# Fewer shapes of the matmul array: spreads on 64 rows, a last layer on 128 rows, and some fp32 matmuls cut into strips

## The reference

```
x = group_norm(x); q,k,v = 1x1 convs(x); x = softmax(q k^T * s) v, projected, + x      # layer 0, one head, 1024 x 1024 scores
h = group_norm(x); q,k,v with 8 heads of 16; x = concat(softmax(q k^T) v) wp + x       # layer 1, eight heads
h = instance_norm(x); q,k,v = 1x1 convs(h); x = x + softmax(q k^T * s) v               # layer 2, one head
Q,K (16 channels), V = 1x1 convs(x); Qn,Kn = l2norm over channels                      # layer 3, linear attention
out = gamma * (sum_n V + Qn (Kn V)) / (N + Qn . (sum_n Kn + eps))
```

## Time and profile before

| | us |
|---|---|
| median of 3 runs | 6187.2 |
| the runs | 6186.3 to 6193.7 |
| the profiled execution, its own time | 6179.8 |
| its span (first to last instruction) | 6178.0 |

### The profile page before, as it was taken

The page is one execution under the profiler, slowest core; times in us unless marked ns, Lnnn a source line. Parts: engine busy times, 40 slices in busy tenths (PEclk is TensorE's granted clock), DMA queues, the critical chain, the costliest instruction groups (busy, mean ns, idle before and its releaser), DMA issues.

```text
span 6178.0 us, 82441 instructions
## 1 busy us (share of the span) xinstructions
PE 5741.7 (93%) x28818; PEld 2690.0 (44%) x28818; DVE 4620.2 (75%) x5748; ACT 4141.6 (67%) x5764; POOL 3426.0 (55%) x2739
## 2 busy tenths in 40 slices
PE   5789999999999999999999999999999999999885
PEld 2334444444444444444444444444444444444332
DVE  2677777777777777777777777777777777777752
ACT  2367777766777676777766767767677777677652
POOL 4336655556665555655555666555565555566433
PEclk7899999999999999999999999999999999999996
DMA  1011101011101101111101110110110110111000
GB/s 36 4 27 24 29 21 30 20 31 24 31 19 30 31 20 31 24 25 25 29 21 31 24 31 19 30 30 21 31 24 21 29 30 20 31 24 31 16 17 8
DMA packets 103485, 154.27 MB, mean 25 GB/s; under 512 B 63776, under 2 KB 66080, under 8 KB 102944
## 3 DMA queue, kind: packets, MB, share of 16 engines
q1 hardware_dynamic: 103072, 149.00, 11.1%
HBM read 18.13 MB, written 16.78 MB: 6 GB/s over the span
## 4 chain that ended last, share of the span: by engine, by line
PE 72%; DVE 16%; ACT 5%; issue 3%; POOL 3%; DMA 0%; SPq 0%; DVEq 0%; POOLq 0%; ACTq 0%
PE p_max L1251 16%; PE p_chain L1251 15%; PE p_sc L1251 12%; PE p_full L1251 11%; PE p_acc L1251 9%; PE p_head L1251 8%; DVE mx_half L1066 8%; ACT p L930 3%; DVE f2mx L1061 2%; DVE fp L1107 2%; POOL x L787 1%; POOL fsum L781 1%; POOL fp_lo L760 1%; DVE f_num L1125 1%; DVE t_dn L1198 1%
## 5 line engine op out<-in xcount | busy, mean ns | idle before, releaser
L1066 DVE TENSOR_REDUCE mx_half<-p_max 128x2 f32<-128x1024 f32 x2048 | 2506.8, 1224 | 891.1 <-PE p_max L1251 883.1
L930 ACT ACTIVATE p<-p_head 128x1024 f32<-128x1024 f32 x2048 | 2094.8, 1023 | 1103.0 <-PE p_head L1251 1047.8
L760 POOL TENSOR_TENSOR fp_lo<-fp,fp_hi 128x512 fp32r<-128x512 f32 x1024 | 1311.6, 1282 | 734.1 <-ACT fp L894 732.5
L781 POOL TENSOR_TENSOR fsum<-fsum,fp 128x512 f32<-128x512 f32 x768 | 987.9, 1286 | 282.3 <-ACT fp L894 282.1
L1251 PE MATMUL p_max<-ks,qs 63*128 63x512 f32 x4096 | 993.9, 481 | 102.0 <-DVE mx_half L1066 80.3
L1251 PE MATMUL p_acc<-p,v 128*17 128x512 f32 x8192 | 1080.9, 601 | 7.8 <-ACT p L930 7.6
L1251 PE MATMUL p_head<-qs,ks 64*128 64x512 f32 x4096 | 938.9, 454 | 43.6 <-ACT p L930 26.5
L892 ACT ACTIVATE fp_hi<-fp 128x512 fp32r<-128x512 f32 x1024 | 641.4, 626 | 367.3 <-DVE fp L1107 261.6
L1107 DVE TENSOR_TENSOR fp<-p_sc,f_shifts 128x512 f32<-128x512 f32 x1024 | 700.1, 684 | 147.5 <-PE p_sc L1251 60.3
L1251 PEld LDWEIGHTS p_max<-ks,qs 63*128 63x128 f32 x4096 | 385.8, 185 | 921.5 <-DVE mx_half L1066 736.3
L1251 PEld LDWEIGHTS p_head<-qs,ks 64*128 64x128 f32 x4096 | 385.7, 185 | 679.5 <-issue 385.8
(11 more groups left out here) (187 smaller groups left out, 7977.6 us busy)
## 6 DMA issues: line engine op xcount, KB each, us to landing
qs<-cq_hi SPq DMA_DIRECT2D x128, 256.0 KB, 4.8
ks<-ck_hi SPq DMA_DIRECT2D x128, 256.0 KB, 4.7
x_in<-x_dram SPq DMA_DIRECT2D x32, 512.0 KB, 4.4
qs<-cq_lo SPq DMA_DIRECT2D x64, 256.0 KB, 4.4
ks<-ck_lo SPq DMA_DIRECT2D x64, 256.0 KB, 5.1
out_dram<-x SPq DMA_DIRECT2D x32, 512.0 KB, 5.3
o<-o SPq DMA_DIRECT2D x256, 32.0 KB, 2.0
zrow<-rz SPq DMA_DIRECT2D x128, 16.0 KB
```

Of the source, the lines that this page charges most:

```text
L760: pool.tensor_tensor(fp_lo[u % 2][:, :], fp[u % 2][:, :], f32(fp_hi[u % 2][:, :]), ALU.subtract).then_inc(f.plo, 1)
L781: pool.tensor_tensor(dst, dst, fp[u % 2][:, :], ALU.add).then_inc(f.sum, 1)
L930: act.activation(p1[slot][:, 2 * pr:2 * pr + 2, :], P_HEAD[:, :].rearrange("p (e n) -> p e n", e=2), ACT.Exp, scale=float(DH) ** -0.5).the ...
L1066: dve.reduce_max(mx_half[:, pr, :, t, kh], P_MAX[:, :].rearrange("p (e n) -> p e n", e=2), AX.X)\
```

## The change

1. `f_spread` and `o_spread` now take 64 rows (the rest of zrow and of the weights `spread_r` is zero), in the same shape as `m_max` and `s_scores`. Both one-head layers share one row (64) of zrow, so `f_return` waits for the other layer's last spread.
2. The last layer: `t_matrix` computes its 17x129 result four times, into the four column strips. `t_turn` transposes four token tiles at once (each padded to 32 columns), so it is two full matmuls of 128 columns and one use of P_CHAIN, and `t_turned` is one copy. A new POOL step `t_spots` makes four masked copies of the matrix, 128x512, and `t_out` is four full matmuls of 128 columns for each half.
3. `mm32`: a full fp32 matmul is issued as four matmuls on the four column strips where the matmul ahead of it was in column strips, and as before elsewhere.
4. P_SC gets a counter of reads like P_CHAIN's.
5. All of TIME is new, with PERIOD 205.92 instead of 206.0.

```diff
-FULL_ROW = {0: 64, 2: 96}
-PERIOD = 206.000
+SUM_ROW = HEAD_ROWS
+STRIP = 32
+PERIOD = 205.920
...
-    m_max=[-78.166, -74.172, -72.387, -66.848, -65.308, -64.707, -61.817, -60.589, -58.987,
...
+            def mm32(dst, lhsT, rhs):
+                if tiling[0] != "columns":
+                    return mm(dst, lhsT, rhs)
+                for j in range(C // STRIP):
+                    strip = slice(STRIP * j, STRIP * (j + 1))
+                    last = mm(dst[strip, :], lhsT[:, strip], rhs, tiles="columns")
+                return last
...
             def o_spread(b, h):
-                mm(P_CHAIN[:, :], spread_r[:, :], zrow[0:SPREAD, half(h)]).then_inc(sem.o_rb, 1)
+                mm(P_CHAIN[:, :], spread_r[0:HEAD_ROWS, :], zrow[0:HEAD_ROWS, half(h)], tiles="rows")\
+                    .then_inc(sem.o_rb, 1)
...
             def f_spread(b, h, layer):
-                f, r = full(layer), slice(FULL_ROW[layer], FULL_ROW[layer] + 2)
+                f, r = full(layer), slice(HEAD_ROWS, 2 * HEAD_ROWS)
-                mm(P_CHAIN[:, :], ones_r[r, :], zrow[r, half(h)]).then_inc(f.rb, 1)
+                mm(P_CHAIN[:, :], spread_r[r, :], zrow[r, half(h)], tiles="rows").then_inc(f.rb, 1)
...
             def t_matrix(b):
                 for t in range(T):
-                    last = mm(P_CHAIN[0:D3 + 1, 0:C + 1], ka[:, t, :], tm[:, t, 2 * D3:W3 + 1],
-                              start=t == 0, stop=t == T - 1)
+                    for j in range(G1):
+                        last = mm(P_CHAIN[STRIP * j:STRIP * j + D3 + 1, 0:C + 1], ka[:, t, :],
+                                  tm[:, t, 2 * D3:W3 + 1], start=t == 0, stop=t == T - 1,
+                                  tiles="columns")
...
-            def t_turn(b, h):
-                for t in range(T // 2):
-                    last = mm(P_CHAIN[0:D3 + 1, tile(t)], t_dn[:, 4 * h + t, :], mat("ident"))
+            def t_turn(b):
+                for h in range(2):
+                    last = mm32(P_CHAIN[:, tile(h)],
+                                t_dn[:, 4 * h:4 * h + 4, :].rearrange("p t d -> p (t d)"),
+                                mat("ident"))
...
             def t_out(b, h):
-                mm(P_CHAIN[:, :], ma[:, 0:C], qt3[:, 4 * h:4 * h + 4, :]).then_inc(sem.t_o, 1)
+                pe.wait_ge(sem.t_sp, b.at(PER.t_sp, 1))
+                for j in range(G1):
+                    last = mm32(P_CHAIN[:, tile(j)], ma_spots[:, j, :], qt3[:, h, :])
+                last.then_inc(sem.t_o, 1)
...
+            def t_spots(b):
+                pool.wait_ge(sem.chain, chain_left("t_keep", b))
+                pool.tensor_tensor(ma_spots[:, :, :],
+                                   ma.rearrange("p (a c) -> p a c", a=1).broadcast_to([C, G1, C]),
+                                   strips[:, :].rearrange("p (j a) -> p j a", a=1)
+                                   .broadcast_to([C, G1, C]), ALU.mult).then_inc(sem.t_sp, 1)
```

More of the change, by code:

```diff
@@ L54 @@
     t_project=(range(3),), t_tokens=(range(3),), t_norms=(), t_keys=(), t_matrix=(), t_keep=(),
-    t_ksum=(), t_scale=(), t_turn=(range(2),), t_turned=(range(2),), t_out=(range(2),),
+    t_spots=(), t_ksum=(), t_scale=(), t_turn=(), t_turned=(), t_out=(range(2),),
     t_leave=(range(2),), store=())
 TIME = dict(
[L59 to L64, removed]
@@ new lines @@
+    o_recip=[602.088, 671.352],
+    o_return=[498.504, 562.776],
+    o_move=[489.144, 552.48],
+    o_spread=[669.48, 671.04],
+    o_divide=[675.72, 679.464],
+    o_project=[674.472, 677.28],
+    o_residual=[682.584, 686.016],
+    i_stat=[689.448],
+    i_apply=[690.384],
+    f_out=[823.608],
+    t_project=[835.152, 837.96, 839.52],
+    t_tokens=[828.6, 832.032, 834.528],
+    t_norms=[837.648],
+    t_keys=[842.64],
+    t_matrix=[854.496],
+    t_keep=[845.76],
+    t_spots=[855.12],
@@ L181 @@
+    t_ksum=[856.056],
+    t_scale=[848.256],
+    t_turn=[863.856],
+    t_turned=[858.864],
+    t_out=[865.728, 869.472],
+    t_leave=[867.6, 868.848],
+    store=[798.648])
 CHAIN_READER = dict(g_average="g_var", p_average="p_var", f_qk="f_hi", p_qk="p_hi",
@@ L250 @@
     f_base = 2
-    f_based = 2
-    f_less = 2 * T
     f_sc = 2 * T
@@ L325, in __init__ @@
         self.base = new(f"f{layer}_base")
-        self.based = new(f"f{layer}_based")
-        self.less = new(f"f{layer}_less")
         self.sc = new(f"f{layer}_sc")
@@ L881, in f_exp @@
                 f = full(layer)
-                act.wait_ge(f.less, b.at(PER.f_less, u + 1))
+                act.wait_ge(sem.sc_read, sc_left("f_less", b, u, layer))
                 if u >= 2:
@@ L1286, in f_value @@
                 for t in range(T // 2):
-                    last = mm(P_CHAIN[:, tile(t)], src[:, tile(4 * h + t)],
+                    last = mm32(P_CHAIN[:, tile(t)], src[:, tile(4 * h + t)],
                               mat("wv0" if layer == 0 else "wv2"))
@@ L1300, in p_value @@
                 for t in range(T // 2):
-                    last = mm(P_CHAIN[:, tile(t)], hx[:, tile(4 * h + t)], mat("wv1"))
+                    last = mm32(P_CHAIN[:, tile(t)], hx[:, tile(4 * h + t)], mat("wv1"))
                 last.then_inc(sem.p_v, 1)
@@ L1320, in m_max @@
                     r = head_rows(e, SHIFT_ROW)
-                    last = mm(P_MAX[:, half(e)], qs[r, pr, tile(t)], ks[r, pr, half(kh)])
+                    last = mm(P_MAX[:, half(e)], qs[r, pr, tile(t)], ks[r, pr, half(kh)],
+                              tiles="rows")
                 last.then_inc(sem.m_s, 1)
```

328 lines of the change are left out of this document (177 added, 151 removed), and 48 rows, old and new, of tables (m_max, m_max_read, s_exp, s_scores).

## The result

| | median us | runs | range |
|---|---|---|---|
| before | 6187.2 | 19 | 6181.1 to 6193.7 |
| after | 6199.4 | 19 | 6177.5 to 6213.5 |

After against before is 1.0019, 95% interval 1.0013 to 1.0026: 0.19% slower, where the forecast was 1% faster. 6,199 lies outside the predicted range. The runs of after also differ more among each other (36 us) than those of before (13 us).

What follows compares the result with a forecast made beforehand. The prediction took PE as the bound. Shapes -75, transposes -41 and waits +46 gave -70 us, counted as -59 in the middle and -5 at the ends: 6,187.2 to 6,123 us, range from a little under 6,071 to 6,190.

Steps and rivals of the forecast that it cites:

- The new order's waits: PE's waits for readers of PSUM tiles, mainly P_MAX: shortfalls rise from 365 to 404, costing +46 us.
- Shapes and transposes: On PE, fewer changes of shape save 75 us and the last layer's four-token t_turn saves 41 us.
- Waits: The +46 us term for PE's waits on PSUM readers, scaled from waits seen of 13.3 us per image.
- t_matrix, t_out, mm32, t_spots, t_keep: Last-layer steps, fp32 strips and the new POOL step: each taken to add 0 us.
- A: Rival for the whole kernel: all 116 us come through and waits don't grow, 6,071 us; chance 0.17.
- B: Rival: DVE's reads of P_MAX set the pace, time stays at 6,187 or reaches 6,232 us; chance 0.19.
- C: Rival: t_matrix is bound by issue at 0.077 us a pass, 6,224 us; chance 0.06 together with D.
- D: Rival: strips of mm32 run one after the other, +160 us, 6,283 us; chance 0.06 together with C.
- The case's own range: The main forecast's narrower range, 6,092 to 6,152 us, explained as half of +46 more or none of it.

Runs made afterwards that it cites:

- e1: The changed kernel with one number moved, so VectorE takes o_recip(1) after m_neg(0) and one f_less instead of ahead of them: 6127.1 us.
- e4: The changed kernel with every fp32 matmul of mm32 in one piece, none in column strips: 6221.4 us.
- e7: e1 with every fp32 matmul of mm32 in one piece, none in column strips: 6154.7 us.
- e14: e2 with every fp32 matmul of mm32 in one piece, none in column strips: 6160.3 us.
- e2: The changed kernel's code with the whole time table of the kernel before: 6154.2 us.
- e5: The changed kernel with the first m_max of the second half moved behind f_pv(11): 6208.6 us.
- e6: e1 with the first m_max of the second half moved behind f_pv(11): 6158.5 us.
- e3: The kernel before with o_recip(1) taken ahead of one f_less and m_neg(0) on VectorE: 6247.5 us.
- e9: The changed kernel with o_recip(1) behind m_neg(0), one f_less and the second half's first mx_half, and both o_spread later: 6145.1 us.

## Why the prediction was wrong

**The step that failed is "The new order's waits".** I summed, for each PSUM tile, how far the next use on PE stands from the last, and took that for all that a new order can do. I had sums over the PSUM tiles and none over the transfers: nothing asked where in DVE's order `o_recip(1)` now stands against `m_neg(0)`, although the order of that engine was there to be read. The earlier trace rows held its tile's waits alone. Two things are missing there, 72 us together. The first is the wait for the gather of `zt`, 1.88 us of DVE's time in the image shown and up to 29 us of the total. The second has no term at all in the prediction: I read "full granted clock" in the earlier trace rows as a property of the middle, and a new order can lose it. Its loss made the other 43 us or more. With that one number moved (e1) the kernel took 6127.1 where 6,123 was forecast, and 180.6 us between most stores, which is what 182.8 less 2.2 gives.

**That agreement is in part two errors that cancel.** *Shapes and transposes:* -116 forecast, 3.6 us per image. PE's busy time fell by 2.5 per image (176.0 to 173.5), about -80. The experiments put most of the excess on the price of a change of shape, 0.07 to 0.17 us instead of 0.20. That figure came from distances between starts in one stretch of a timeline; that a change costs less where PE waits anyway may be the reason, and wasn't tested. *Waits:* +46 forecast for the middle and ends, 1.4 per image; PE's idle time rose from 6.9 to 7.5, about +19. PE's own waits in the middle rose from 130 to 151 us. The scale of this term was a remainder, too: 13.3 us of waits per image, where by the earlier trace rows PE is idle for 6.9.

*t_matrix, t_out, mm32, t_spots, t_keep:* 0 forecast for all. `t_matrix` 1.77 as forecast; POOL's `t_spots` is waited for by nobody. PE's wait for `t_dn`, 16.5 us in the middle of before, is gone in after and e1; the prediction had seen it and set it against a cost of `t_keep`. e4, e7 and e14 say that the strips save what their shapes save, or a little more.

**Rivals.** A (full gain) didn't come in any kernel. B was nearest in kind: it gave DVE's queue as the way to a slower kernel, `f_less` held up behind an earlier entry. It named P_MAX's reads as that entry, at 109 us. The real one was an entry that waits for a DMA. Its probability of slower was 0.07. C is refuted by the rows of `t_matrix`, D by the strips' 1.04 us for a group.

**The chances.** I gave 0.13 to slower. Every case had been worked out at a constant clock, so no range could hold what happened. The case's own range, 6,092 to 6,152, doesn't follow from the reason given for it either: half of +46 more gives 6,146, and none of it 6,077.

## To carry to other kernels

When an order is changed, look on every engine for an entry that waits for a transfer and has moved ahead of one that the bounding engine needs; a sum over tiles doesn't see it. Read a full clock as a state that the present order keeps up, and put a price on its loss wherever a change lets TensorE stand for a microsecond or two in every image. Before a new order is judged, move such an entry back by itself: here one number of over 600 was worth more than the rest of the change.

## What the runs showed of the hardware

**The clock.** In before, e2 and e14 TensorE's clock stayed at 2.4 GHz for the whole middle. In after it fell behind stands of 0.2 to 0.7 and 1.6 to 2.1 us, the starts behind them 3 to 3.5 us apart, in nearly every image; in e5 behind one of 2.3 to 2.4 us in nearly every image, and in e6 behind one of 1.8 in most. But in e3 it fell in four of 24 images, with 1.7 to 1.8 us in one piece in most of them, and in e9 five times, four of them with no stand over 0.9 us near. What else decides isn't settled. A fall lasts from 3.4 to 13.7 us in the records. The spread of after's 19 runs, 36 us, goes with their granted clock (0.969 in the fastest, 0.962 in the slowest).

**VectorE beside GpSimd.** The reciprocal's last operation has 32 elements per partition. It took 0.19 us in before, where POOL was idle, and 1.20 us in after, where POOL worked on

```profile
3164.05 1.27 POOL L812 TENSOR_TENSOR fsum<-fsum,fp 128x512 f32<-128x512 f32 x1 [1.54 <-ACT fp L934]
3165.29 1.27 POOL L791 TENSOR_TENSOR fp_lo<-fp,fp_hi 128x512 fp32r<-128x512 f32 x1
```

and it ended within 0.05 us of POOL's second operation here (3165.40 + 1.20 against 3165.29 + 1.27). The cast ahead of it (0.54 for 0.18) ended with POOL's first, and `m_both` took 0.53 for 0.19. The Trainium skill's page "SBUF — State Buffer" (section "🔬 SBUF: two separate sides") says that the two share one pair of ports as an exclusive lock, among others for a VectorE operation with two SBUF inputs against one of GpSimd that reads SBUF. The trace agrees for L1183 and `m_both`, which have two, and for the reciprocal (L1178), which has one and took its usual 0.35 beside POOL. The cast has one input and was held up too; the case of two inputs doesn't explain that. In e1, where L1183 took 1.22 us, this extra second is most of what PE's stand of 1.28 us behind `mx_half` is made of.
